# Making the ternary scales, the first ternary weights and the layer 2 rotation tables earlier, and a new order of layer 2's attention steps

## The reference, cut to what matters

```
# layer 1, attention: 16 heads of 32, queries and keys normalised per head, a second attention over 16 keys
# layer 1, feed forward
def ternary_quant(w):
    scale = jnp.mean(jnp.abs(w)) + EPS
    q = jnp.clip(jnp.round(w / scale), -1.0, 1.0) * scale
    return w + jax.lax.stop_gradient(q - w)
up     = x @ ternary_quant(W_up).T        # 512 -> 2048
gate   = x @ ternary_quant(W_gate).T      # 512 -> 2048
out    = (silu(up) * gate) @ ternary_quant(W_down).T
# layer 2, attention: 32 heads of 16, queries and keys turned by angles pos * freq (axial rope)
ang = pos[..., :, None] * freqs ; cos = jnp.cos(ang) ; sin = jnp.sin(ang)
out = stack([x1 * cos - x2 * sin, x1 * sin + x2 * cos])
```

## Time and profile before

| | us |
|---|---|
| median of three runs | 3756.95 (3756.22 to 3761.6) |
| profiled execution, its own time | 3756.28 |
| its span | 3753.3 |
| experts | about 775 to 1245 |
| layer 1 attention | about 1245 to 1697 |
| fence 3 passed | 1702.6 |
| ternary feed forward | to 2113.5 |
| layer 2 attention | 2113.6 to about 2633 |
| PE busy | 3414.0 (91%) |

### The profile page before, as it was taken

The page is one execution under the profiler, slowest core; times in us unless marked ns, Lnnn a source line. Parts: engine busy times, 40 slices in busy tenths (PEclk is TensorE's granted clock), DMA queues, the critical chain, the costliest instruction groups (busy, mean ns, idle before and its releaser), DMA issues.

```text
span 3753.3 us, 62066 instructions
## 1 busy us (share of the span) xinstructions
PE 3414.0 (91%) x23446; PEld 2808.3 (75%) x23446; DVE 2365.9 (63%) x4621; ACT 1667.5 (44%) x3641; POOL 1307.8 (35%) x1239
## 2 busy tenths in 40 slices
PE   7999999959999699987999699997789999999977
PEld 6999999937777456656998545554689999999865
DVE  6677777863323488865443456665667777777766
ACT  5666665521111255542222255554245555555431
POOL 1013334112243588732222346665422222222212
PEclk9999999979999899998999989999889999999989
DMA  3236665024644100002000100000000000000001
GB/s 129 82 137 228 222 222 180 29 112 157 254 154 172 71 24 25 11 5 79 35 23 1 37 3 4 3 4 15 31 7 13 18 18 18 18 7 19 12 1 48
DMA packets 94869, 246.53 MB, mean 66 GB/s; under 512 B 14448, under 2 KB 18672, under 8 KB 89840
## 3 DMA queue, kind: packets, MB, share of 16 engines
q1 hardware_dynamic: 88336, 222.12, 16.9%
q0 software_dynamic: 6240, 20.45, 1.5%
HBM read 364.95 MB, written 70.52 MB: 116 GB/s over the span
## 4 chain that ended last, share of the span: by engine, by line
PE 39%; DVE 6%; issue 3%; POOL 2%; ACT 2%; DMA 0%; SPq 0%; POOLq 0%; DVEq 0%; ACTq 0%
PE banks L104 35%; PE banks L214 4%; ACT P L78 1%; POOL kst L87 0%; DVE xn L92 0%; DVE X L87 0%; DVE st L270 0%; DVE PL L87 0%; DVE X L95 0%; POOL rs L87 0%; DVE KL L95 0%; ACT nkT L81 0%; DVE P L91 0%; POOL CL L87 0%; DVE XL L87 0%
## 5 line engine op out<-in xcount | busy, mean ns | idle before, releaser
L87 DVE TENSOR_TENSOR X<-X,banks 128x512 f32<-128x512 f32 x352 | 240.2, 683 | 189.3 <-PE banks L104 188.9
L98 DVE TENSOR_REDUCE nmx<-banks 128x4 f32<-128x1024 f32 (+2 forms) x256 | 239.3, 956 | 158.1 <-PE banks L104 155.0
L104 PE MATMUL banks<-XH,wqh 128*128 128x256 f32 x1024 | 291.4, 285 | 0.0
L104 PE MATMUL banks<-XL,wqh 128*128 128x256 f32 x1024 | 285.8, 279 | 0.0
L104 PE MATMUL banks<-XH,wql 128*128 128x256 f32 x1024 | 285.6, 279 | 0.0
L104 PE MATMUL banks<-XH,tT 128*128 128x256 f32 x1024 | 248.8, 286 | 13.7 <-issue 6.6
L87 POOL TENSOR_TENSOR slo<-sraw,shi 128x512 fp32r<-128x512 f32 x96 | 126.8, 1321 | 376.4 <-ACT shi L81 352.8
L78 ACT ACTIVATE nPT<-banks 128x1024 f32<-128x1024 f32 x192 | 196.1, 1021 | 129.8 <-PE banks L104 129.4
L104 PE MATMUL banks<-XL,tT 128*128 128x256 f32 x1024 | 247.3, 285 | 0.0
L104 PE MATMUL banks<-woh,OH 128*128 128x512 f32 x512 | 219.2, 428 | 11.6 <-DVE OL L87 10.0
L78 ACT ACTIVATE P<-banks,nb,qst 128x256 f32<-128x256 f32 x256 | 141.3, 561 | 190.7 <-DVE nb L87 190.6
(11 more groups left out here) (433 smaller groups left out, 10500.2 us busy)
## 6 DMA issues: line engine op xcount, KB each, us to landing
WU<-expert_parts SPq DMA_DIRECT2D x39, 4096.0 KB
WD<-expert_parts SPq DMA_DIRECT2D x39, 2048.0 KB
sraw<-in_moe_w SPq DMA_DIRECT2D x96, 256.0 KB, 3.1
expert_parts<-shi SPq DMA_DIRECT2D x96, 256.0 KB
expert_parts<-slo SPq DMA_DIRECT2D x96, 256.0 KB
wqr<-in_L_xattn_Wq SPq DMA_DIRECT2D x16, 512.0 KB, 4.3
wor<-in_L_xattn_Wo SPq DMA_DIRECT2D x16, 512.0 KB, 5.4
sraw<-in_L_ffn_factors SPq DMA_DIRECT2D x32, 256.0 KB, 3.0
```

The lines of the kernel that those rows point to most:

```text
L87: return self.e.tensor_tensor(out, a, b, op)
L98: return self.e.tensor_reduce(out, a, AX.X, op, **kw)
L104: return self.e.matmul(out, l, r, start=start, stop=stop, skip_group_check=skip)
```

## The change

Five things are done.

1. **Scales** are made in the experts: a step `size` in block 8 for the reduction and a piece ("size", 0) in block 10 for PE's sum and the four small operations.
2. **First ternary weights** in layer 1: SP loads raw parts 0 and 1 there, into places of their own, and DVE makes part 0 at a new step `make` between the add of tile 13 and the add of tile 14.
3. **A drain** of POOL in layer 1, ahead of its add of tile 13.
4. **Layer 2's loads and angles** in the ternary feed forward: the weights when the last raw part is taken and when the third group's `up` are done; the angles on DVE behind `down 25`, cosine and sine on ACT behind `up 31`. The tiles are laid out anew for it, with two buffers for the reduced angles.
5. **Layer 2's order**: other `PLACES`, and shifts of their own for the first four tiles.

```diff
-    KEYS = {3: ("dv", 0), 5: ("dk", 0), 24: ("k", 0), 28: ("k", 1)}
+    KEYS = {3: ("dv", 0), 5: ("dk", 0), 10: ("size", 0), 24: ("k", 0), 28: ("k", 1)}
...
+            if j == 8:
+                yield "size", 0
...
+            if step == "size":
+                dve.wait_ge(S["pk1"], 3)
+                dve.wait_ge(S["size"], 48)
+                dve.red(self.W["t"]["s3"][:, 0, :], self.s48[:].rearrange("p (w g) -> p w g", w=3), ALU.add).then_inc(S["tscale"], 1)
...
-            "out": (48.5, 51.5), "add": 54, "stat": 95.5, "gl": -116.5, "ga": -94, "gn": -82.5, "gt": -74,
+            "out": (48.5, 51.5), "add": 54, "make": 30, "stat": 95.5, "gl": -116.5, "ga": -94, "gn": -82.5, "gt": -74,
...
-        2: {"ps": (2, 3, 5, 7.5, 8, 11, 13, 15), "st": (0, 2, 5, 7, 8.5, 10.5, 12.5, 14),
-            "s": (-11, -9, -7.5, -5, -3, -0.5, 2, 3.5), "pv": (6, 9.5, 13, 16), "div": (12, 17.5), "mt": (-3.5, 5),
-            "k0": (-27.5, -20), "k1": (-25.5, -16), "q0": (-22, -17), "q1": (-24, -17), "q2": (-18.5, -13),
-            "k2": (-15.5, -14), "q3": (-17.5, -8), "k3": (-15, -5), "kp": -49.5, "krd": -50, "krp": -44.5,
-            "qp": (-41, -39), "qrd": -39, "qrp": -37, "vp": -20, "vb": -18.5, "out": (35, 35.5), "add": 36, "stat": 37.5}}
+        2: {"ps": (2, 3, 5, 8.5, 10, 11, 12.5, 14), "st": (0, 2, 5, 6.5, 8.5, 10.5, 12.5, 14),
+            "s": (-10, -9, -7.5, -5, -3, -0.5, 2, 3.5), "pv": (6, 9.5, 13, 16), "div": (11.5, 16.5), "mt": (-3.5, 5),
+            "k0": (-28, -20.5), "k1": (-28, -20), "q0": (-24.5, -18), "q1": (-22, -17), "q2": (-18.5, -13.5),
+            "k2": (-16, -14), "q3": (-18, -8), "k3": (-15, -5), "kp": -50, "krd": -49.5, "krp": -39.5, "qp": (-41, -39),
+            "qrd": -39.5, "qrp": -36, "vp": -20, "vb": -19, "out": (34.5, 37), "add": 35.5, "stat": 45.5,
+            "q1st": (-3, 0, -1, 0), "k1st": (-8, 2, 0, 1), "low1": (-12, -0.5, -1, 0), "lowq1": (-4.5, 0, 0, 0)}}
...
     def pe_key(self, pe, kind, t, z):
-        if kind == "k":
+        if kind == "size":
+            pe.wait_ge(S["tscale"], 1)
+            pe.mm(z[:, 0:3], self.ones[:], self.W["t"]["s3"][:, 0, :]).then_inc(S["pe_one"], 1)
+        elif kind == "k":
...
+            dve.ts(scale, z[:, 0:3], 2.0 ** -20, 1e-8, ALU.mult, ALU.add).then_inc(S["tscale"], 1)
+            dve.wait_ge(S["tscale"], 2)
+            dve.ts(half, scale, 0.5, None, ALU.mult).then_inc(S["tscale"], 1)
+            dve.ts(nhalf, scale, -0.5, None, ALU.mult).then_inc(S["tscale"], 1)
+            dve.tt(sgd, scale[:, 1:2], scale[:, 2:3], ALU.mult).then_inc(S["tscale"], 1)
...
     def sp_narrow_load(self, sp, L):
...
+            sp.wait_ge(S["tern"], 96)
+            sp.dma(w["wq"][:], self.ins[pre + "Wq"]).then_inc(S["n_wq"], 16)
+            sp.wait_ge(S["tup"], 96)
+            sp.dma(w["wkv"][:], self.ins[pre + "Wkv"]).then_inc(S["n_wkv"], 16)
             sp.dma(w["pos"][:], self.ins["fside_BxSx2_0"].rearrange("b (t p) c -> p (b t) c", p=128)).then_inc(S["load_a"], 16)
-            sp.dma(w["wkv"][:], self.ins[pre + "Wkv"]).then_inc(S["n_wkv"], 16)
-            sp.dma(w["wq"][:], self.ins[pre + "Wq"]).then_inc(S["n_wq"], 16)
...
+    def sp_make_early(self, sp):
+        S, w = self.S, self.W["t"]
+        sp.wait_ge(S["n_vv"], NT)
+        sp.wait_ge(S["dq1"], 4 * NT - 3)
+        for r in range(2):
+            sp.dma(self.raw_parts(r)[0], self.ins[self.FFN1[r]][0]).then_inc(S[f"raw{r}"], 16)
...
+            if step == "add" and l1 and t == NT - 3:
+                pool.e.drain()
...
+    def act_angles(self, act):
+        S, w = self.S, self.W[2]
+        for c, name in enumerate(("cosT", "sinT")):
+            act.wait_ge(S["ang"], 11 + 7 * c)
+            act.act(w[name][:].rearrange("p t c -> p (t c)"), w[f"rr{c}"][:], ACT.Sin).then_inc(S["act_one"], 1)
...
-            if c:
-                dve.wait_ge(S["act_one"], ONE["cos"])
...
-        else:
-            self.dve_angles(dve)
         for step, t in w["steps"]:
+            if step == "make":
+                self.dve_make(dve, 0)
...
         yield "turn", 1
-        yield "make", 0
         yield "norm", 2
...
+                if u == 31:
+                    self.act_angles(act)
...
+                if u == 25:
+                    self.dve_angles(dve)
...
         self.fence(sp, 4)
         sp.count_on(NARROW_1)
-        self.sp_narrow_load(sp, 2)
```

More of the change, by code:

```diff
@@ L1583, in first @@
         def first(kind, n):
[L1585 to L1589, removed]
+            for shift, kinds in (("rows1", "gl ga gn gt"), ("q1st", "qp qb qsq qst qrd qrp"), ("qsc1", "qsc"),
+                                 ("k1st", "kp kb ksq kst ksc krd krp"), ("low1", "k0 k1 k2 k3"), ("lowq1", "q0 q1 q2 q3")):
+                if kind in kinds.split() and n < len(at.get(shift, ())):
                     return at[shift][n]
@@ L1610, in narrow_list @@
                     put(16 * t + at[kind] + first(kind, t), kind, t)
-        order = ("mix gl ga gn gt st ps s pv out kp qp vp add kb qb vb krd qrd div krp qrp ksq qsq kst qst ksc qsc "
+        order = ("mix make gl ga gn gt st ps s pv out kp qp vp add kb qb vb krd qrd div krp qrp ksq qsq kst qst ksc qsc "
                  "mt k2 q2 k3 q3 k0 q0 k1 q1 stat").split()
@@ L1614, in narrow_list @@
             put(16 * 15, "mix", 0)
+        else:
+            put(16 * 15 + at["make"], "make", 0)
         steps = [] if L == 1 else [("ln", NT - 1)]
@@ L2227, in act_narrow @@
         U, SC = w["U"], w["SC"]
-        if not l1:
-            for c, name in enumerate(("cosT", "sinT")):
-                act.wait_ge(S["ang"], 11 + 7 * c)
-                act.act(w[name][:].rearrange("p t c -> p (t c)"), w["rr"][:], ACT.Sin).then_inc(S["act_one"], 1)
         z7 = banks[7][:].rearrange("p (c n) -> p c n", c=4)
@@ L2516, in ternary_tiles, with raw_parts, dve_make @@
         sb("hf", [128, 2, 512], F32)
-        sb("s3", [128, 6, 3], F32)
-        self.W["t"] = w
+        assert self.top == self.arena + 63488
+        sb("neg", [128, 512], F32)
+        sb("raw0", [128, 4, 512], F32)
+        w["first1"] = self.at("tfirst1", [128, 4, 512], F32, self.top)
+        sb("T0", [128, 2, 4, 512], F32R)
+        w["s3"] = self.at("ts3", [128, 6, 3], F32, self.W["e"]["end"] + 256)
+        self.W["t"] = w
+    def raw_parts(self, r):
+        w, g = self.W["t"], r // 3
+        raw = w["first1" if r == 1 else f"raw{r % 2}"][:]
+        return raw, w[f"T{r % 3}"][:, 1 - g % 2 if r % 3 == 0 else g % 2, :, :]
+    def dve_make(self, dve, r):
+        S, w = self.S, self.W["t"]
+        half, nhalf = w["s3"][:, 2, :], w["s3"][:, 3, :]
+        g, W = r // 3, r % 3
+        raw, taken = self.raw_parts(r)
+        dve.wait_ge(S["tscale"], 5)
+        dve.wait_ge(S[f"raw{r % 2}"], 16 * (r // 2 + 1))
+        if g >= 2 and W == 2:
+            dve.wait_ge(S["tdown"], 16 * (g - 1))
+        elif g >= 2:
+            dve.wait_ge(S["tup"], 4 * (8 * (g - 2) + 7) + 3 + W)
+        for c in range(4):
+            dve.wait_ge(S["tern"], 8 * r + 2 * c)
+            dve.ts(w["neg"][:], raw[:, c, :], nhalf[:, W:W + 1], None, ALU.is_lt).then_inc(S["tern"], 1)
+            dve.wait_ge(S["tern"], 8 * r + 2 * c + 1)
+            dve.stt(taken[:, c, :], raw[:, c, :], half[:, W:W + 1], w["neg"][:], ALU.is_gt, ALU.subtract).then_inc(S["tern"], 1)
     def sp_ternary(self, sp):
@@ L2522, in sp_ternary @@
         for step, r in self.ternary_steps():
-            if step == "make":
+            if step == "make" and r > 1:
                 sp.wait_ge(S["tern"], 8 * (r - 1))
-                sp.dma(w["raw"][:, r % 2, :, :], self.ins[self.FFN1[r % 3]][r // 3]).then_inc(S[f"raw{r % 2}"], 16)
+                sp.dma(self.raw_parts(r)[0], self.ins[self.FFN1[r % 3]][r // 3]).then_inc(S[f"raw{r % 2}"], 16)
+        self.sp_narrow_load(sp, 2)
     def pool_ternary(self, pool):
```

97 lines of the change are left out of this document (45 added, 52 removed).

## The result

The changed kernel takes **3719.06 us** (median of 4 runs, 3710.3 to 3722.74) against 3756.89 in the runs beside it: a ratio of 0.9895, 95% interval 0.9881 to 0.991. A second series gave 3718.64 against 3760.42, ratio 0.9903 (0.9881 to 0.9925). The profiled execution has a span of 3721.0 us against 3753.3.

What follows compares the result with a forecast made beforehand. PE, busy 91% of the span, was taken to bound the kernel. From 3756.28 us, -9.8 + 0.4 + 0.45 - 10.3 - 2.8 - 2.3 = -24.4 gave 3731.9, say 3732 us, range 3723 to 3742.

Steps and rivals of the forecast that it cites:

- Seam one: Fence 3: earlier fence opening 3.2, scales 1.48 and early make of weight 0 5.1 us, 9.8 us saved in all.
- rival (a): POOL's drain at fence 3 stays long, its debt not paid once: +5.3 us, 3737; chance 0.10.
- Rival (f): The make in layer 1's tail delays `out` by as much as it saves, needing 8 us; chance 0.02.
- Experts: Making the scales in the experts costs PE a pair of matmuls: +0.4 us (bounds 0.3 and 1.5).
- Angles: Angles on DVE in the feed forward's unit 26 make a later add late: +0.45 us (bounds 0 and 3.0).
- Fence 4: With weights, angles and tables ready, PE starts layer 2's first projection at 2114.95, not 2125.25: 10.3 us saved.
- Rival (b): Layer 2's first `krd` is held by POOL's memset as the angles were: +3.2 us, 3735; chance 0.08.
- The new order: Layer 2's start: first projection to first scores in 27.7 us, not 30.5: -2.8 us (bounds 0 and -4.5).
- rival (e): New order costs in every layer 2 pair: 3741 with `q0` alone, chance 0.05; 3763 with both `q0` and `krp`, 0.03.
- The clock: Layer 2's start: first half-clock stretch goes, -2.3 us; the second, behind ACT's table load, stays.
- Rival (d): Full clock through layer 2's start as fence 4's hole shrinks: first projection -1.5, second slow stretch -5.6 us, 3725; chance 0.12.
- Rival (c): Clock goes on falling in layer 2's start and the order gains nothing: +2.3 + 2.8 us, 3737; chance 0.10.

Runs made afterwards that it cites:

- no_drain: Changed kernel without POOL's early drain in layer 1; 3727.64 us, ratio 0.9921 to the kernel before.
- after_3: The changed kernel, no edits, run and profiled once more; 3729.76 us in one run.
- scales_loads: Kernel before plus only scales made in the experts and first two weights loaded in layer 1; 3754.59 us against 3760.22, ratio 0.9984.
- order_old: Changed kernel with the old order of steps in layer 2, weights, angles and tables still early; 3738.12 us, ratio 0.9947 to the kernel before.
- angles_late: Changed kernel with layer 2's loads, angles, cosine and sine behind fence 4 again; 3733.74 us, ratio 0.994 to the kernel before.
- old_dense: Changed kernel with layer 2's old order, the waits of its start filled with matmuls nobody reads; 3732.1 us, ratio 0.9932 to the kernel before.
- l1_filled: Changed kernel plus unread matmuls in layer 1's start: 11 in the hole behind fence 2, 3 in the wait for `nstq`; 3726.13 us, ratio 0.9916.
- filled: Changed kernel with layer 2's loads and angles behind fence 4 again, 8 unread matmuls in that hole; 3731.51 us, ratio 0.992.

## Why the prediction was right or wrong

**Seam one, -9.8 forecast: right.** The early drain took 7.2 us and the one at the fence 1.36, DVE was the last at the fence, and no_drain brought DVE's wait of 5.4 us back; so the debt is paid once, and rival (a) falls. The drain began at 1690.7, 0.3 us ahead of DVE's add of tile 13 (1690.97), where I had it 0.5 us behind that add (1685.6 and 1685.07): everything here stands 5.9 us later on the clock of this execution, most of it from the long start of layer 1. Counted from that add or from the fence the whole chain came as forecast, down to the `up` that waits for part 1, 11.8 us behind the fence (11.7). The make cost 2.0 us in the tail (2.1; in after_3 the tail is 3.1 us longer still, with the last `out` at half clock) and saved 5.3 behind the fence (5.1); the scales 1.7 in the feed forward's rest (1.48), in the one comparison that has them and the loads alone. The rests say -2.7 and -5.7 for layer 1 and the feed forward, against -3.2 and -6.1. Rival (f) falls: the make saved 5 us and cost 2.

**Experts, +0.4: within what can be told.** Rest +1.0 in the means of three, scattered by 1 to 2 us, and none in scales_loads.

**Angles, +0.45: small, as forecast.** DVE's timeline of the changed kernel, to set beside the earlier trace rows:

```profile
2037.46 0.55 DVE L92 TENSOR_SCALAR xn<-X,mv,rs 128x512 f32<-128x512 f32 x1 [0.73 <-POOL rs L87]
2037.92 0.45 DVE L91 TENSOR_SCALAR ang<-npos 128x32 f32<-128x32 f32 x4
...
2042.33 0.74 DVE L95 SCALAR_TENSOR_TENSOR thf<-banks,ts,tsl 128x512 f32<-128x512 f32 x1
...
2045.08 0.68 DVE L87 TENSOR_TENSOR X<-X,banks 128x512 f32<-128x512 f32 x1
```

From the norm to the add it is 7.62 us, 7.46 before: 0.16 late. The angles take 4.4 us there.

**Fence 4, -10.3: right.** 10.0 by the rests (order_old against the kernels with both undone), 9.9 by angles_late.

**Rival (b): refuted.** The first `krd` ran at 2114.45 in the usual 0.43 us while POOL's memset (2112.66 to 2116.17) went on. The Trainium skill, page "SBUF — State Buffer", section "SBUF: two separate sides", names as those that ask for the shared pair the operations of DVE in a two-port mode and, only against a GpSimd operation that reads SBUF, those with two SBUF inputs; this one has a PSUM input, and the trace agrees with the rule. Of the four operations on the positions in the earlier trace rows the trace of before has two at some 0.2 us, done before that memset began, and two that lasted 3.7 us, until it ended; those two were held, not all four.

**The new order, -2.8 forecast, -8.1 measured in the rests: the step that failed first.** 4.4 of it lie in the start (rests: 73.3 to 74.2 us in five kernels with both undone, 69.3 with the new order, 63.8 with the early angles, 58.9 to 59.7 with both), inside the bound of 4.5 that I had written down and not taken. The way from first projection to first scores, which I had replayed as 27.7 us, took 26.2. PE's waits in the start fell from 16.5 to 12.9 us beside hole and fence. The other 3.7 lie behind the start, where I had put 0 by comparing the two lists "for a steady pair": true for that pair (28.3 and 28.2 us), and the 29.21 us busy of 30 are those of the earlier trace rows, so rival (e) falls. But the last three pairs are no steady pairs. They went from 25.3, 25.1, 24.1 to 24.4, 24.4, 23.2 us. What PE waited for in the last three pairs, before and then after (us in total, times, longest):

```profile
PE banks L104 <- DMA nqT<-nmT: 5.4, 4, 2.2
```

```profile
PE banks L104 <- DMA nqT<-nmT: 2.7, 3, 1.6
```

In both kernels the scores wait there for the DMA that brings the row maxima, and in the new order they wait half as long; PE's other waits differ by 0.4 us in all, so this one makes up the 2.5 us. Which of the moved places does it is not shown: `mt` did not move, and the first `s` stands a place later. I never read this stretch.

**The clock, -2.3 forecast, -9.4 over the span and -10.6 in layer 2: the larger failure.** The link was right as far as the experiments go: the stretch behind the wait-ridden transpositions goes when the order is denser, and old_dense supports it. The size was not: I credited the first of the falls only and kept the second, on the ground that ACT's table load stays. The table load did stay, and the fall behind it went in the three profiles with 2.6 us lost (it came back, smaller, in after_3, with 9.6, and in three experiments). Over all profiles, seven with the changed layer 2 and five with the old one, the loss goes from 15.3 to 5.8; like with like the order has some 5.5 of that. The rest may be the closed hole's or chance; the profiles do not separate the two, and my sum had no term for either. A part also lies behind the start (2.8 to 4.5 us lost there before, 1.1 to 1.3 after), where I had looked for none. Rival (d) had the right number (3725, and 22.5 us for the start against 23.0) for the wrong reason: it tied the falls to the hole, and with the hole closed and the old order the start loses 12.2 us; and the first projection, which it had at 2.0 us, still took 3.38. Rival (c) falls, as the order did gain. What I should have priced is the whole loss of the start, which the windows view gives at once: 9.9 us in the profile I had, all of it at stake when the order of the start changes; and I should have taken more than the one profile, as the same start lost 13.0 to 13.6 in three of four others.

**Outside the sum**: layer 1 and the experts moved by up to 10 us between two profiles of one kernel, in either direction. The range of 19 us was drawn from my terms alone and held none of this scatter. The medians of two series (3719.06 and 3718.64) are below it all the same; the one execution of after_3, 3729.76, is inside.

## What to carry to other kernels

When a change makes PE's work denser at a place where the granted clock falls, price two things separately: the waits that go, and the sum of busy time times (1 - clock) over the whole stretch up to where the clock is steady, as something that may go altogether, read from more than one profile. A drain of POOL may hold a debt that can be paid earlier, beside other work. Look at the ends of a loop as at stretches of their own: an order judged on the steady pair is not judged on the first and the last.

## What the runs showed of the hardware

POOL's drain of 7.8 us at fence 3 is neither its last add (1.26 us) nor tied to the fence: put 12 us ahead it took 7.2 us there, and the later one then took 1.36. What it waits for is not shown; it is the first drain behind the experts.

In the one profile of each experiment, keeping PE busy in a hole did not protect the clock behind it. In l1_filled PE worked 11.41 us without a break and lost 12.3 us in the start all the same; in filled the clock was at 0.95 or more from 4 us behind the fence on, through the hole, and fell 56 us behind the fence. Filling the short waits between small matmuls went with a much smaller loss (12.2 to 2.8 us in layer 2, 12.3 to 3.1 in layer 1). And a higher clock need not gain anything: the projection of 3.70 in place of 5.40 us was followed by a wait of 4.39 in place of 2.66, behind which the clock fell, and that start was 4.6 us longer. With the same order of instructions the start of layer 2 lost 1.4 us in three profiles and 5.8 to 8.4 in four others, so a time forecast from one profile carries some us of that in every stage of this kind.
